# Half-size loads of the next batch's Q and K stacks, placed between the row transfers, with a new order of phases

## The reference

```
x = x + 0.5 * ffn(layernorm(x))      # first FFN
x = x + attention(layernorm(x))      # 16 heads of 8 channels, rotary q and k
x = x + 0.5 * ffn(layernorm(x))      # second FFN, same weights

ffn(x):       relu(x @ Wq1.T + b1) @ Wq2.T + b2, with 512 hidden units;
              Wq = clip(round(W / (mean|W| + 1e-5)), -1, 1)
attention(x): q, k, v = x @ W.T + b; q, k rotated; softmax(q k / sqrt(8)) v; @ Wo.T + bo
```

## Time and profile before

| | us |
|---|---|
| three runs | 551.0, 543.98, 550.92; median 550.92 |
| the profiled execution | 548.73, its span 546.6 |
| PE busy | 498.3 (91%) |
| DVE busy | 392.0 (72%) |
| ACT busy | 369.1 (68%) |
| GpSimd busy | 213.8 (39%) |
| mean granted clock of the PE | 0.975 |

### The profile page before, as it was taken

The page is one execution under the profiler, slowest core; times in us unless marked ns, Lnnn a source line. Parts: engine busy times, 40 slices in busy tenths (PEclk is TensorE's granted clock), DMA queues, the critical chain, the costliest instruction groups (busy, mean ns, idle before and its releaser), DMA issues.

```text
span 546.6 us, 12209 instructions
## 1 busy us (share of the span) xinstructions
PE 498.3 (91%) x4981; PEld 233.6 (43%) x4981; DVE 392.0 (72%) x582; ACT 369.1 (68%) x440; POOL 213.8 (39%) x286
## 2 busy tenths in 40 slices
PE   7887869979999999999999996999799988999986
PEld 5654523432453435353535332433234333433445
DVE  4578558766888688778787884868767886788324
ACT  2767457885858685867676764777576767667751
POOL 3315057336454283447351744145612731103202
PEclk9999779998999999999999997999989999999999
DMA  8054015602370129003620344024701380000000
GB/s 272 8 203 106 1 27 192 134 2 73 122 157 3 42 98 229 7 26 113 181 55 22 118 135 101 2 60 156 156 2 41 123 208 3 22 2 3 3 20 20
DMA packets 18967, 44.44 MB, mean 81 GB/s; under 512 B 2400, under 2 KB 5472, under 8 KB 17888
## 3 DMA queue, kind: packets, MB, share of 16 engines
q1 hardware_dynamic: 18240, 43.14, 28.5%
q10 hardware_dynamic: 672, 0.52, 0.3%
HBM read 20.58 MB, written 18.87 MB: 72 GB/s over the span
## 4 chain that ended last, share of the span: by engine, by line
PE 69%; ACT 10%; DVE 6%; issue 4%; DMA 4%; POOL 2%; SPq 0%; ACTq 0%; POOLq 0%; DVEq 0%
PE heads_acc L565 22%; PE unit L550 14%; PE unit L535 11%; PE side L629 8%; ACT probs L767 7%; DMA q_stack<-max_T 4%; DVE maxima L874 3%; PE side L604 3%; PE side L621 2%; ACT hidden L757 2%; PE side L614 2%; PE side L599 2%; PE side L584 1%; PE side L589 1%; ACT heads L773 1%
## 5 line engine op out<-in xcount | busy, mean ns | idle before, releaser
L874 DVE TENSOR_REDUCE maxima<-unit 128x2 f32<-128x1024 f32 x256 | 304.4, 1221 | 89.5 <-PE unit L535 88.5
L767 ACT ACTIVATE probs<-unit 128x1024 f32<-128x1024 f32 x256 | 255.8, 1023 | 100.9 <-PE unit L550 99.8
L565 PE MATMUL heads_acc<-probs,v_heads 128*32 128x512 f32 x1024 | 137.9, 611 | 0.9 <-ACT probs L767 0.9
L550 PE MATMUL unit<-q_stack,k_stack 64*128 64x512 f32 x512 | 116.1, 469 | 22.6 <-DMA q_stack<-max_T 11.6
L535 PE MATMUL unit<-k_stack,q_stack 62*128 62x512 f32 x512 | 108.7, 444 | 4.3 <-ACT probs L767 2.4
L550 PEld LDWEIGHTS unit<-q_stack,k_stack 64*128 64x128 f32 x512 | 47.4, 186 | 100.1 <-ACT probs L767 39.6
L1067 POOL TENSOR_SCALAR max_parts<-maxima 128x16 fp32r<-128x16 f32 x32 | 6.5, 204 | 182.0 <-DVE maxima L874 182.0
L535 PEld LDWEIGHTS unit<-k_stack,q_stack 62*128 62x128 f32 x512 | 48.9, 190 | 59.4 <-issue 22.6
L629 PE MATMUL side<-w_q,hidden 128*32 128x128 f32 (+1 forms) x1472 | 53.9, 276 | 2.7 <-ACT hidden L757 2.7
L629 PEld LDWEIGHTS side<-w_q,hidden 128*32 128x32 f32 (+1 forms) x1472 | 46.0, 114 | 13.3 <-issue 10.5
L565 PEld LDWEIGHTS heads_acc<-probs,v_heads 128*32 128x32 f32 x1024 | 21.9, 108 | 37.0 <-issue 30.1
(11 more groups left out here) (160 smaller groups left out, 464.3 us busy)
## 6 DMA issues: line engine op xcount, KB each, us to landing
k_scratch<-k_parts SPq DMA_DIRECT2D x16, 512.0 KB, 3.4
q_scratch<-q_parts SPq DMA_DIRECT2D x16, 512.0 KB, 3.4
k_stack<-k_scratch SPq DMA_DIRECT2D x14, 512.0 KB, 7.1
q_stack<-q_scratch SPq DMA_DIRECT2D x14, 512.0 KB, 9.2
resid<-in_x SPq DMA_DIRECT2D x8, 256.0 KB, 5.2
k_swap<-k SPq DMA_DIRECT2D x14, 128.0 KB, 2.3
q_swap<-q SPq DMA_DIRECT2D x14, 128.0 KB, 2.3
out_y<-resid SPq DMA_DIRECT2D x7, 256.0 KB, 2.1
```

The source lines that it names most:

```text
L550: mm = pe.matmul(to[:, e, :], k_stack[part, quad // NQ % 2, pair, kt * P:(kt + 1) * P], q_stack[part, quad // NQ % 2, pair, :], start=True ...
L565: mm = pe.matmul(heads_acc[32 * j:32 * j + 32, :], v_heads[:, b % 2, at, ODD * odd:ODD * odd + 32], probs[:, burst % RING, j, :], start=(k ...
L767: act.activation(probs[:, burst % RING, 2 * pp:2 * pp + 2, :], unit_of(USE_OF["exp", n]), ACT.Exp, scale=SCALE).then_inc(s_exp, 1)
L874: dve.tensor_reduce(maxima[:, quad % 2, :, r], unit_of(USE_OF["max", k]), AX_X, ALU.max).then_inc(s_max, 1)
```

## The change

The loads of the next batch's stacks are cut in two by pairs of heads: each `stack` call now loads four pairs, four DMAs of 256 KB. The first half is issued behind the rows of the third quad, the second behind those of the fourth. Each half has a semaphore of its own, for even and odd batches, and the PE waits before a quad for the half in which it lies. Two of the `set_rows` for slot 1 leave the twelve steps and become tokens of phase 0, of which there are now six (`rows0` to `rows5`, in `ROWS_LATE`). `ffn1_stats@5` moves in phase 0 from before the first `e` to behind the twelfth. The tokens of both texts stand in a new order.

```diff
--- before.py
+++ after.py
@@ -55,70 +55,70 @@
 
 
 PE_FIRST = """
-attn_T@1 ffn1_stats@5 e
+e attn_T@1 m
 e m k@1 m
-e
-e m q@1
-e m ffn1_T m pv m
-e ffn1_up0 m max_T1
-e m ffn1_up1 m m rows0 ffn1_up2 pv m m pv
+e m q@1 m ffn1_T
+e m m
+e max_T1
+e m m ffn1_up0 rows0 m
+e ffn1_up1 m pv ffn1_up2
+e pv
 e m ffn1_up3
 e
-e ffn1_down0
+e ffn1_down0 m
+e ffn1_stats@5 rows1 m ffn1_down1 rows3 rows2 ffn1_down2 ffn1_down3 m m
+e max_T2 pv pv
+e m pv m attn_stats pv m rows5
+e pv
+e v rows4
 e m
-e ffn1_down1 ffn1_down2 rows3 rows2 m ffn1_down3 pv attn_stats
+heads_copy0 e pv
+e heads_T0 m
+e attn_T m
+e m
+e max_T3
+e m pv m m pv
 e
-e pv
-e m pv m max_T2 pv m
-e m rows1 m pv
-heads_copy0 e m v
+e pv m
+e pv m
 e
+e pv k
+e m
+e pv max_T4 m
+e m q m pv
 e
-e attn_T m pv m
-e
-e pv m max_T3
-e heads_T0
-e m
-e
-e
-e m
-e m pv k m m pv q
-e m
-e max_T4 pv m
-e pv
-e m pv
 """
 PE_STEADY = """
 m ffn1_T e m pv
-heads_copy1@-1 ffn1_up0 e m ffn1_up1
-e m heads_T1@-1
+heads_copy1@-1 ffn1_up0 e m ffn1_up1 m
+e heads_T1@-1
+e
+e m pv ffn1_up2
+e m ffn1_stats@5 m max_T1 pv
+e m out_T pv ffn1_up3 m
+e out
 e m
-e pv ffn1_up2
-e m ffn1_stats@5 pv max_T1
-e m m out_T pv ffn1_up3 m
-e out
+e pv ffn1_down0
+e ffn2_stats m ffn1_down1
+e ffn1_down2 m
+e m ffn1_down3 pv m attn_stats
+e pv max_T2 m
 e
-e m pv ffn1_down0
-e ffn1_down1 ffn2_stats
-e m m ffn1_down2 ffn1_down3
-e m pv m
-e pv attn_stats max_T2 m
-e
-e v pv m ffn2_T
-e pv m
-heads_copy0 e m ffn2_up0
-e m ffn2_up1
-e pv heads_T0
-e m m ffn2_up2
+e v pv m
+e ffn2_T
+heads_copy0 pv e m ffn2_up0
+e m m ffn2_up1 pv heads_T0
+e m ffn2_up2
+e m
 e pv max_T3
 e m m ffn2_up3 pv
-e m ffn2_down0 m m
-e ffn2_down1 ffn2_down2 ffn2_down3
+e m ffn2_down0 m
+e m ffn2_down1 ffn2_down2
 e m
-e pv attn_T
-e
-e m k pv
-e m m max_T4 pv
+e ffn2_down3 pv attn_T
+e m
+e pv k
+e m m pv max_T4
 e m q
 e m pv
 """
@@ -181,6 +181,7 @@
               11: first_ffn("down", 3, 0)[2:4]}
 MAX_T_BEFORE = 9
 OPEN_ACC = 7
+ROWS_LATE = [(0, "k", 1), (0, "q", 1), (1, "k", 0), (1, "k", 1), (1, "q", 0), (1, "q", 1)]
 OPEN_BANK = {use[0]: use[3] for use in PROLOGUE if use[0][0] in "qk"}
 
 FILL = {("ffn1_up", 0, 0): 6, ("attn_T", 0, 0): 38, ("k", 0, 0): 3, ("ffn1_T", 0, 2): 8, ("ffn1_up", 0, 2): 8}
@@ -305,7 +306,7 @@
         s_rope = {n: sem(f"{n}_rope_steps") for n in "qk"}
         s_scratch = {n: sem(f"{n}_scratch_landed") for n in "qk"}
         s_stack_first = sem("first_quad_landed")
-        s_stack = [sem(f"stack_landed_{k}") for k in ("even", "odd")]
+        s_stack = [sem(f"stack_landed_{k}") for k in ("even_first", "even_second", "odd_first", "odd_second")]
         s_v_psum = sem("v_in_psum")
         s_v = sem("v_heads_filled")
         s_scores = sem("scores_in_psum")
@@ -384,7 +385,9 @@
 
         def stacked(j, g):
 
-            return (s_stack_first, STACK_LANDED) if j == 0 and g == 0 else (s_stack[j % 2], (j // 2 + 1) * STACK_LANDED)
+            if j == 0 and g == 0:
+                return s_stack_first, STACK_LANDED
+            return s_stack[2 * (j % 2) + g // 2], (j // 2 + 1) * STACK_LANDED
 
 
         last = B - 1
@@ -458,6 +461,7 @@
 
             def to_scratch(n, j):
                 if j > 1:
+                    sp.wait_ge(*stacked(j - 2, 1))
                     sp.wait_ge(*stacked(j - 2, NQ - 1))
                 for c in range(PARTS):
                     sp.wait_ge(s_rope[n], j * ROPE_STEPS + ROPE_STEPS - PARTS + c + 1)
@@ -485,7 +489,8 @@
             to_scratch("k", 0)
             to_scratch("q", 0)
             stack(0, slice(0, 2), s_stack_first)
-            stack(0, slice(2, NPAIR), s_stack[0])
+            stack(0, slice(2, NPAIR // 2), s_stack[0])
+            stack(0, slice(NPAIR // 2, NPAIR), s_stack[1])
             max_row(0)
             for b in range(B + 1):
                 if b == 0:
@@ -497,10 +502,14 @@
                     max_row(b * NQ + 1)
                 if on("values", b):
                     to_scratch("q", b + 1)
-                    stack(b + 1, slice(0, NPAIR), s_stack[(b + 1) % 2])
                 if b < B:
                     max_row(b * NQ + 2)
+                if on("values", b):
+                    stack(b + 1, slice(0, NPAIR // 2), s_stack[2 * ((b + 1) % 2)])
+                if b < B:
                     max_row(b * NQ + 3)
+                if on("values", b):
+                    stack(b + 1, slice(NPAIR // 2, NPAIR), s_stack[2 * ((b + 1) % 2) + 1])
                 if 0 < b < B:
                     sp.wait_ge(s_y, b)
                     sp.dma_start(out[b - 1].rearrange("(p t) d -> p t d", t=T), batch_rows(b - 1)).then_inc(s_stored, 16)
@@ -817,15 +826,13 @@
                     side_part(use)
                 if k in (2, 3):
                     set_rows(1, 0, "kq"[k - 2], 0)
-                if k in (7, 8):
-                    set_rows(1, 0, "kq"[k - 7], 1)
             n = 0
             for use in work(ACT_PLANS):
                 if use[0] == "e":
                     exps(n)
                     n += 1
                 elif use[0] == "rows":
-                    set_rows(1, 1, "kkqq"[use[1]], use[1] % 2)
+                    set_rows(1, *ROWS_LATE[use[1]])
                 elif use[0] == "heads_copy":
                     take_heads(use[2] * 2 + use[1])
                 else:
```

## The result

The changed kernel takes 524.68 us in the median of four runs (523.54 to 526.57), the kernel before 549.43 (543.98 to 551.0). The ratio is 0.957, interval 0.949 to 0.965: 4.3% faster. The forecast was 531, range 522 to 543. Runs more than 1.5% above the fastest of their kernel count as slow and are left out of every ratio.

What follows compares the result with a forecast made beforehand. The PE, busy 91% of the span, was taken as the bound. Terms 13 + 2.5 + 6.0 - 2.5 = 19 took 548.7 to 529.7 us; half of a 2.2 us run offset made it 531, range 522 to 543.

Steps and rivals of the forecast that it cites:

- the rows' wait: Batches 4 to 6: rows issued ahead of the stack loads end 10.4 us of PE wait; with clock, 13 us gained.
- The clock: Batches 4 and 5, after the waits for rows: 4.4 and 3.4 busy us at half speed cost at most 2.2 + 1.7.
- The halves: Stack loads: first half lands 8.1 us after third transpose, 21st score step at 11.8; cost nothing, cover 3.7 us.
- Rival D: First half late for the 21st score step: 28 us lost against a gain of 19, 558 us; chance 0.05.
- Before phase one: Twelve score steps: two settings of constant rows leave, ending a PE wait and low clock; gain 2.5 us, bounds 0 to 3.4.
- Phase one: Moved statistics and the fourth quad's wait gain 8.2 us, two more settings of rows lose 2.2; net 6.0 us.
- The settings of rows: Phase one: two more settings, 3.8 us of ACT, only partly hidden; loss 2.2 us, bounds 0 to 3.8.
- The statistics: Phase one: moving batch 5's statistics behind step 11 gains 3.8 us of wait and 2.0 of clock, at most 3.0.
- Phases placed anew: New token order: 0.3 us late in each of seven batches, 2.1, plus 0.4 ending batch 6; loss 2.5 us.
- The chain that was named: Second FFN, transpose to first up part needing the split: 0 to 2.0 us late per batch, 2.1 in seven.
- C: Rows in batches 4 to 6 land late for another reason than the stacks; about 544 us, chance 0.09.
- B: Gain given back in ACT and the shared bank: phase one nets 3, split late by 5.6 us; 540 us, chance 0.24.

Runs made afterwards that it cites:

- filled_waits: Kernel before, with small matmuls of ones in the PE's waits for the third quad's rows in batches 4 to 6: 548.84 us, ratio 0.997.
- whole_behind: Changed kernel with stacks loaded whole again (four DMAs of 512 KB), issued behind the third quad's rows: 561.45 us, ratio to before 1.021.
- rows_back: Changed kernel with two settings of constant rows back behind steps 7 and 8 of the twelve, not in phase 0: 527.56 us.
- rows_in_gaps: Changed kernel with two settings of constant rows behind steps 10 and 11 of the twelve, the last two behind steps 22 and 23: batch 0 61.5 us from first transposed score.
- both_behind: Changed kernel with both halves issued behind the third quad's rows, the second not held back for the fourth quad's: 524.28 us.
- stats_back: Changed kernel with the statistics of batch 5 ahead of the first exponential again: 532.66 us.
- steady_before: Changed kernel with the old steady order of phases 1 to 7 (`PE_STEADY`): 527.19 us.
- halves_only: Kernel before with only the loads cut in halves, behind the third and fourth quad's rows: 542.32 us, ratio 0.988.
- split_early: Changed kernel with GpSimd's split of the second quad's maxima ahead of the end of k's rotation in phase 0: time unchanged, no figure given.
- filled_split: Changed kernel with 14 small matmuls of ones in the PE's wait for the second quad's split: batch 0 2.5 us shorter, not shown in the median.
- stacks_ahead: Changed kernel with both halves issued ahead of the third quad's rows: 539.44 us, ratio to before 0.984.

## Why the prediction was right, step by step

**What bounds the kernel, and the rows' wait: right.** 13 us were taken for batches 4 to 6, 14.5 came off; putting the loads back costs 12.8 by the stretches and 14.8 by the medians, and the cut alone on the old kernel brings 13.7. The waits of 10.4 us and the clock behind them, 1.7 and 1.3, make 13.4; the rest goes to the new order and to chance. The 3.2 us floor was real: in batch 7 the score waits 0.6 us and comes 3.2 after the transpose. In batch 5 the rows took 4.1 us, so 0.6 us of wait is left there as well, and the sign "under 1" was missed with 1.2.

**The clock: busy time counts, and half of it is too much.** With the 6.8 us stretch of batch 4 at low clock the loss was 1.7 us. The PE was idle for 2.4 us of that stretch. Its 4.4 busy us cost 1.7, the 3.4 of batch 5 cost 1.3, and the 6.6 of batch 6 in filled_waits cost 2.5: 0.37 to 0.40 us for each, where the prediction took a half (2.2 and 1.7) as the most. Why it is less than a half no run shows. The Trainium skill (TensorE: Matmul & The Clock Gate, "HAM oscillation") takes half of the throttled time; that gives 3.4, 1.7 and 3.4 in these three, where the runs show 1.7, 1.3 and 2.5.

**The halves: right in kind, with less room than was thought.** A transfer took 4.9 us from issue to landing in the median, as taken, but the one that counts is the last of the four, with 4.6 to 6.3. The half lands 8.6 to 8.9 us after the transpose and not 8.1, the step comes at 11.6 (11.8 were taken), and 2.7 to 3.0 us are left, not 3.7 (3.6 in batch 5, and in batch 0 only 1.2). The Trainium skill (DMA: Bandwidth & Descriptors, "Anatomy of one DMA") has about 2.0 us of a transfer fixed, in a fit for transfers that GpSimd issues. As an estimate, from 9.2 us for the whole that would be 5.6 for a half; the profile has 4.9, for transfers issued in fours by SyncE. Rival D was no idle one. The rest of it, that a landing later than 11.8 us turns the change into a loss, is what whole_behind shows.

**Before phase one: right, a little small.** 3.5 us against 2.5, just over the bound of 3.4. The slow stretch at 61.5 us is gone, and rows_back brings the loss back (3.7).

**Phase one: the sum was too high.** 6.0 taken, 4.1 found. The settings of rows were put at a loss of 2.2. Taking two of them out wins 2.1 to 3.3 us in rows_back from the first transposed score on, with less low clock, and nothing in rows_in_gaps with the same low clock; so ACT's part in it is most likely small, and how small stays open. The statistics are worth 3.5 to 4.7 by the stretches (5.8 taken): their wait of 3.8 and less than 1 of clock. The step that failed is "up to 3.0 for the busy part of the slow stretch; I take 2.0": the slow stretch did not go. With DVE free the PE ran on into the next wait, for GpSimd's split of the second quad's maxima, 1.6 us, and the clock fell at 73.3 us instead of 75.2, for the same 6.8 us. The fourth quad's wait did go, but another slow stretch of 3.4 us at 104.0, behind a 1.45 us wait for ACT, took the place of the one at 122.9. In both_behind the same wait is there and no low clock after it, and batch 0 is 1.2 us shorter:

```profile
103.31 0.49 PE L559 MATMUL unit<-q_stack,k_stack 64*128 64x512 f32 x2 [1.45 <-ACT probs L776]
```

```profile
103.80 0.50 PE L559 MATMUL unit<-q_stack,k_stack 64*128 64x512 f32 x2 [1.43 <-ACT probs L776]
```

**Phases placed anew: the sign was wrong.** A loss of 2.5 us was taken; the new steady order gains about one. The chain that was named costs about what was said (1.7 us in seven waits of up to 0.2 for the split, 2.1 taken; up parts also wait 1.7 for `attn_out`, 0.2 before), but the many short waits that the order removes elsewhere were not counted.

**What the prediction had no step for.** 1.8 us between the two profiles lie ahead of the first stack load, where the change does nothing. In the kernel before, the filling matmuls after the sum of the weights' magnitudes took 0.20 us each, in the changed one 0.12:

```profile
7.61 3.23 PE L638 MATMUL heads_acc<-ones_f 128*128 128x256 bf16 x16
```

```profile
6.82 2.02 PE L647 MATMUL heads_acc<-ones_f 128*128 128x256 bf16 x17
```

Profiles of both sorts occur on either side: 37.3 us to the first load in before, stats_back and steady_before, 35.5 to 35.7 in halves_only and rows_back. The change has no part in it. What sets it is not shown, and it made the forecast look 1.8 us worse than its steps were. The last stretch, 70.8 to 73.1 us whatever the kernel, varies too: 70.8 to 71.4 in the profiles without 3.4 us of low clock before its last microseconds, 72.3 to 73.1 in those with it.

**The number.** The forecast is 6.3 us above the median. The steps gave 19 us where the profiles are 22.2 apart; only half of the 2.2 us between the median and the profiled execution of the kernel before was put on top; and the profiled execution of the changed kernel (526.57) is 1.9 above its median. Against the stretches the steps were 1.0 too small before phase one and 1.5 in batches 4 to 6, 1.9 too large in phase one, and 2.5 were taken off for an order that costs nothing. With the 1.8 of the opening, and -0.5 and -1.1 in batches 1 to 3 and at the end, these partly cancel; so far the nearness of the sum is luck.

**The signs.** Batches 4 to 6 take 52.4, 53.3 and 51.4 us (52 to 53 were named), at a clock of 1.00. Phase one, 62.5 us in the prediction's cut, is 4.1 shorter, so about 58.4, just over the 55 to 58. DVE has no wait for the normalised batch 4 any more. Nothing of C and D appeared, and of B only a trace: one wait of 1.45 us for ACT at the 19th transposed score, behind a setting of rows.

## What to carry to other kernels

A small transfer that the critical engine waits for should be issued ahead of a large one with slack, and the large one must then be checked against its own deadline, in the order of work, from the row that shows how long the last transfer of its first needed part takes: here the same move with an uncut load was slower than doing nothing. Cut a load where its consumer first needs it, not to spread it evenly. When a wait goes, look for the next one within the same few microseconds before you count the clock loss behind it as won.

## What the runs showed of the hardware that was not expected

The low clock does not follow from the length of one wait. With the 1.6 us wait taken out (split_early) the clock still fell in the same place, with only waits of 0.2 to 0.7 us in the 5 us before; with that wait filled by matmuls of ones (filled_split) it did not fall. The wait of 1.4 to 1.5 us for ACT in batch 0 was followed by 3.4 us of low clock in the changed kernel and by none in both_behind and filled_split. The wait of 2.34 us in batch 6 of the kernel before was followed by none, that of 2.27 in stacks_ahead by 3.4 us.

Query-stack transfers issued in fours land in 3.0 us with 128 KB each, in 4.9 with 256 KB and in 8.6 to 9.2 with 512 KB, in the median. The last of the four, for which the consumer waits, takes 4.6 to 6.3 with 256 KB and 9.8 to 12.2 with 512 KB: twice the size, twice the time.

Last, a lower mean clock mostly goes with a longer run: of the kernel before, 544.08 us at 0.978, 551.49 at 0.969 and 561.83 at 0.957, though also 555.21 at 0.975. Its runs lie between 543.98 and 561.83 us, those of the changed kernel between 523.54 and 526.57.
